# AdaLN block with chunked attention and a routed feed-forward: side pieces on two PSUM banks, routing weights spread by the load

## What is computed

```python
h = layernorm(x) * (1 + ca) + sa
# attention: 16 heads of 128, chunks of 64 rows
q, k, v = h @ q_w.T + q_b, h @ k_w.T + k_b, h @ v_w.T + v_b
beta = softplus(h @ b_w.T + b_b)
out = ((l2norm(q) @ l2norm(k).T) * decay_mask) @ (beta * v)      # inside a chunk
x = x + ga * ((out * silu(h @ og_w.T)) @ o_w.T + o_b)
# feed-forward: 16 experts of 176 columns, top 6 of a softmax, and a shared expert of 352
h = layernorm(x) * (1 + cb) + sb
p = softmax(h @ gate_w.T); w = top6(p) / sum(top6(p))            # 0 for the other ten
y = sum_e w[:, e] * swiglu_e(h) + swiglu_shared(h)
x = x + gb * y
```

## Time and profile before

| what | value |
|---|---|
| median of 3 runs | 2330.7 us (2329.98 to 2335.05) |
| the profiled execution, its own time | 2331.89 us |
| span of its trace | 2330.2 us |
| PE busy | 2215.1 us (95%), granted clock 0.986 of full |
| DVE, ACT, POOL busy | 58%, 37%, 24% |
| PE idle before the products of the gates | 26.8 us, 20 times |
| attention loop / feed-forward loop | about 30 to 1486 us / 1486 to 2328 us |

### The profile page before, as it was taken

How to read it: one execution, slowest core, us unless ns; L and a number is a source line. 1 busy time by engine, 2 the same in 40 slices (tenths; PEclk the granted TensorE clock), 3 DMA queues, 4 the chain that set the end, 5 groups by cost and what they waited for, 6 DMA issues and landing times.

```text
span 2330.2 us, 32531 instructions
## 1 busy us (share of the span) xinstructions
PE 2215.1 (95%) x11436; PEld 1852.0 (79%) x11436; DVE 1349.6 (58%) x2299; ACT 872.5 (37%) x1484; POOL 547.6 (24%) x543
## 2 busy tenths in 40 slices
PE   7899899999989998989999999899999999999998
PEld 6788788777877777877888888788878888888887
DVE  4566566655665666566657565455555545545554
ACT  3433434444434443344444333233333332233332
POOL 2234334333433333333434444100000000000000
PEclk8999999999999999999999999999999999999999
DMA  8353441453533535423313221144334323423221
GB/s 290 136 173 124 171 123 40 143 155 102 145 96 118 151 97 159 136 85 113 105 60 113 91 94 70 46 149 145 108 119 158 97 98 112 167 97 113 95 95 59
DMA packets 192768, 276.40 MB, mean 119 GB/s; under 512 B 99184, under 2 KB 132960, under 8 KB 192608
## 3 DMA queue, kind: packets, MB, share of 16 engines
q1 hardware_dynamic: 192608, 274.33, 36.7%
HBM read 214.79 MB, written 59.51 MB: 118 GB/s over the span
## 4 chain that ended last, share of the span: by engine, by line
PE 48%; DVE 2%; issue 1%; ACT 1%; DVEq 0%; ACTq 0%
PE proj_ps L635 24%; PE out_ps L635 8%; PE s_ps L911 3%; PE av_ps L911 3%; PE kt_ps L911 3%; PE qt_ps L911 3%; PE s_ps L833 1%; PE av_ps L842 1%; PE qt_ps L819 0%; DVE sumsq L1326 0%; PE kt_ps L824 0%; DVE gated L1338 0%; PE misc_ps L714 0%; ACT gated_hi L1044 0%; DVE scores L1319 0%
## 5 line engine op out<-in xcount | busy, mean ns | idle before, releaser
L635 PE MATMUL proj_ps<-w_qkv,h_t 128*128 128x512 f32 x2304 | 624.3, 410 | 8.4 <-DVE v_sb L1313 2.3
L635 PEld LDWEIGHTS proj_ps<-w_qkv,h_t 128*128 128x128 f32 x2304 | 417.1, 192 | 97.5 <-issue 17.8
L635 PE MATMUL proj_ps<-h_t,w_qkv 128*128 128x512 f32 x1800 | 443.3, 391 | 0.9 <-DVE acc L1358 0.9
L591 POOL TENSOR_TENSOR inv_norm<-guarded,minus_half 128x8 f32<-128x8 f32 x128 | 209.4, 1636 | 873.2 <-DVE guarded L1330 873.2
L635 PEld LDWEIGHTS proj_ps<-h_t,w_qkv 128*128 128x128 f32 x1800 | 336.0, 188 | 71.5 <-issue 2.8
L1030 ACT ACTIVATE q_t<-qt_ps 128x512 f32<-128x512 f32 x128 | 76.5, 597 | 425.1 <-PE qt_ps L819 424.9
L635 PE MATMUL proj_ps<-h_t,w_gate 128*128 128x512 f32 x768 | 197.7, 408 | 29.0 <-ACT gate L1050 26.8
L635 PEld LDWEIGHTS proj_ps<-h_t,w_gate 128*128 128x128 f32 x768 | 143.1, 193 | 71.4 <-ACT gate L1050 36.7
L1313 DVE TENSOR_TENSOR q_sb<-proj_ps,bias 128x512 f32<-128x512 f32 x128 | 88.3, 690 | 191.3 <-PE proj_ps L635 178.9
L1326 DVE TENSOR_REDUCE sumsq<-squares 128x8 f32<-128x1024 f32 x128 | 155.6, 1216 | 23.5 <-DVE stage L1234 13.4
L635 PE MATMUL out_ps<-gated_hi,w_out 128*128 128x512 f32 x512 | 159.0, 392 | 3.1 <-ACT gated_hi L1044 2.2
(11 more groups left out here) (183 smaller groups left out, 3094.8 us busy)
## 6 DMA issues: line engine op xcount, KB each, us to landing
w_qkv<-tile_scr SPq DMA_DIRECT2D x100, 768.0 KB, 4.3
w_qkv<-head_scr SPq DMA_DIRECT2D x45, 1024.0 KB, 11.0
head_scr<-stage SPq DMA_DIRECT2D x30, 512.0 KB, 3.0
w_gate<-head_scr SPq DMA_DIRECT2D x15, 1024.0 KB, 4.9
w_out<-head_scr SPq DMA_DIRECT2D x15, 1024.0 KB, 6.7
tile_scr<-stage SPq DMA_DIRECT2D x25, 512.0 KB, 3.2
x_in<-_attn_hidden_states_dram SPq DMA_DIRECT2D x16, 512.0 KB, 5.5
h_scr<-stage SPq DMA_DIRECT2D x16, 512.0 KB, 3.2
```

What stands on the lines that cost most here:

```text
L591: pool.tensor_tensor(inv_norm[b][:, :], guarded[b][:, :], minus_half[:, :], ALU.pow).then_inc(inverted, 1)
L635: mm = pe.matmul(out, w, y, start=(j == 0 and m == 0), stop=(3 * j + m == n - 1))
```

## The change

Three things are changed.

- **Two banks.** A chunk in the second place of a unit with `t` 3 or 0 now uses `out_ps`, which the output products leave alone from their read-out in the `t == 2` unit to the next `t == 2` unit. All other chunks keep `misc_ps`. Each bank has a count of its own; the first output product waits for the chunks of `out_ps`, and such a chunk for the adds that read the last output products.
- **No chunk of a weight or of the routing in (n, 1) with `t == 1`**, in front of the gate products. The routing takes the places one after the other and leaves that one out, so from `turn` on its pieces stand one place later. `prep` and `tile` leave it out too. The input of the second supertile of a quarter is started at unit 32q+22 and no longer at 32q+24, by which its `turn` leaves (n, 1) with `t == 1` and its `soft2` enters it.
- **No `spread`.** `wturn`'s 16 rows are stored, and the load repeats each row eight times. The product L681, the copy L992 and the constant are gone; six routings have these in the unit loop and two in the feed-forward loop. `weights_t` lies in `h_f` now.

```diff
-    def route(s, put, at):
-        put(*at(0), "delta", s)
...
-        put(*at(11), "wturn", s)
-        put(*at(12), "spread", s)
+    def route(s, put, places):
+        for task in (("delta", s), ("x1", s, 0), ("x1", s, 1), ("stats", "f", s), ("norm", "f", s), ("turn", "f", s, 0),
+                     ("turn", "f", s, 1), (("split", "f", s), ("logits", s)), ("prob", s), ("pick", s), ("weigh", s),
+                     ("wturn", s)):
+            at = next(places)
+            for part in task if isinstance(task[0], tuple) else (task,):
+                put(*at, *part)
+
+    def from_unit(n):
+
+        while True:
+            yield n, 0
+            if n % TS != 1:
+                yield n, 1
+            n += 1
...
-            route(2 * (q - 1) + a, put, lambda r, n=32 * q - 1 + 8 * a: (n + r // 2, r % 2))
+            route(2 * (q - 1) + a, put, from_unit(32 * q - 1 + 8 * a))
...
-            first_norm(2 * (q + 1) + a, 32 * q + 18 + 6 * a)
-    chunks = ("turn", "beta", "x1", "logits", "wturn", "spread", "prep", "tile")
-    free = lambda n, p: not any(t[0] in chunks for t in side[n, p])
+            first_norm(2 * (q + 1) + a, 32 * q + 18 + 4 * a)
+    free = lambda n, p: (n % TS, p) != (1, 1) and not any(t[0] in CHUNKS for t in side[n, p])
...
+        second = {t for n in range(N) if n % TS in (3, 0) for t in side[n, 1] if t[0] in CHUNKS}
+        bank_at = {t: sum((v in second) == (t in second) for v in list(chunk_at)[:j]) for t, j in chunk_at.items()}
+        side_bank = {t: (out_ps, side_freed[1]) if t in second else (misc, side_freed[0]) for t in chunk_at}
+        added_by = {t: (n + 1) // TS - 1 for n in range(N) for t in side[n, 1] if t in second}
...
-                elif t[0] == "spread":
+                elif t[0] == "wturn":
                     s = t[1]
-                    sp.wait_ge(combined, s + 1)
-                    sp.dma_start(comb_scr[s], comb_out).then_inc(comb_stored, 16)
+                    sp.wait_ge(weights_copied, s + 1)
+                    sp.dma_start(comb_scr[s], weights_t).then_inc(comb_stored, 16)
...
-                    sp.dma_start(combine[q % 2][:, a, :], comb_scr[s]).then_inc(comb_loaded[q % 2], 16)
+                    sp.dma_start(combine[q % 2][:, a, :], comb_scr[s].unsqueeze(1).broadcast_to([E, ER, ST]))\
+                      .then_inc(comb_loaded[q % 2], 16)
...
             def chunk(task):
-                j = chunk_at[task]
-                after(pe, misc_free, j)
+                after(pe, side_bank[task][1], bank_at[task])
+                if task in second:
+                    after(pe, added, 2 * added_by[task])
+                return side_bank[task][0]
...
                 after(pe, added, 2 * i + k)
+                if k == 0:
+                    after(pe, side_freed[1], second_by[min(TS * (i + 1) + 2, N)])
```

More of the change, by code:

```diff
@@ L39 @@
 Q, K, V, G, O = range(5)
+CHUNKS = ("turn", "beta", "x1", "logits", "wturn", "prep", "tile", "final")
 NI = NQ * NG * 2
@@ L125, in plan @@
     for a in range(2):
-        route(2 * (NQ - 1) + a, lambda u, _, *task: late[u].append(task), lambda r, a=a: (2 + 30 * a + 2 * r, 0))
+        route(2 * (NQ - 1) + a, lambda u, *task: late[u].append(task), ((u,) for u in range(2 + 28 * a, NU, 2)))
     for q in range(NQ):
@@ L279, in build @@
         order += [("final", NQ - 1, a, half) for a in range(2) for half in range(2)]
-        CHUNKS = ("turn", "beta", "x1", "logits", "wturn", "spread", "prep", "tile", "final")
         chunk_at = {t: j for j, t in enumerate(t for t in order if t[0] in CHUNKS)}
+        second = {t for n in range(N) if n % TS in (3, 0) for t in side[n, 1] if t[0] in CHUNKS}
+        bank_at = {t: sum((v in second) == (t in second) for v in list(chunk_at)[:j]) for t, j in chunk_at.items()}
+        side_bank = {t: (out_ps, side_freed[1]) if t in second else (misc, side_freed[0]) for t in chunk_at}
+        added_by = {t: (n + 1) // TS - 1 for n in range(N) for t in side[n, 1] if t in second}
+        second_by = [sum(t in second for v in range(n) for p in range(2) for t in side[v, p]) for n in range(N + 1)]
         norm_at = {t[1:3]: j for j, t in enumerate(t for t in order if t[0] == "norm")}
@@ L556, in _ @@
             pool.memset(causal[:, :], 1.0)
-            pool.memset(prob_ext[:, :, E:E + 2], 2.0)
-            pool.memset(spread[:, :], 1.0).then_inc(made, 1)
+            pool.memset(prob_ext[:, :, E:E + 2], 2.0).then_inc(made, 1)
             pool.wait_ge(made, 1)
@@ L675, in do @@
                         mm = pe.transpose(misc[0:E, t * P:(t + 1) * P], picked[:, t, :], ident)
[L676 to L681 removed]
+                    mm.then_inc(side_filled, 1)
                 elif kind == "prep":
@@ L707, in do @@
                     _, q, a, half = task
-                    chunk(task)
+                    misc = chunk(task)
                     for h in range(KC):
@@ L930, in do @@
                 kind = task[0]
+                misc, freed = side_bank.get(task, (None, None))
                 if kind == "turn":
@@ L1122, in do @@
                     if before:
-                        dve.wait_ge(misc_filled, chunk_at[("turn", *before[0], 1)] + 1)
+                        dve.wait_ge(side_filled, chunk_at[("turn", *before[0], 1)] + 1)
                     for t in range(TS):
```

102 lines of the change are left out of this document (37 added, 65 removed).

## The result

| kernel | median | ratio to before, 95% interval |
|---|---|---|
| before (six runs beside the change) | 2331.89 us | |
| changed | 2316.53 us (2313.95 to 2323.69, six runs) | 0.9937 [0.9923, 0.9951] |

The change makes the kernel 0.6% faster, about 15 us. I had forecast 0.9%, 21 us: the sign is right and the gain three quarters of it. The profiled execution took 2316.73 us, with a span of 2315.0.

The account below looks back on a forecast made before the run. PE, busy 2215.1 of 2330.2 us, was taken to bound the kernel. Terms -25 - 9 + 3 + 12 - 1.6 = -20.6 gave 2311.3 profiled, 2310 us median; forecast 2303 to 2318 (0.49), 8-in-10 range 2294 to 2327.

Parts of the forecast that it names:

- preparation, 1 to 4: Weight preparation in units 0 to 6: bank waits partly go, about 2 in units 0/1 included; gain 6.5 us.
- gates without a piece: Gate products with no chunk in front: the Silu comes earlier in six routings and units 5, 9, 17, 21; gain 9 us.
- softplus and what is behind: Softplus of supertiles 3, 5, 7 moves to the gates, costing 8.7 us, while units behind gain; net +3 us.
- routing, the rest of its units: Routing without the spread product, but with everything behind `turn` one place later; net cost +12 us.
- Pieces across a unit boundary: From (n, 1) to (n+1, 0), two banks remove waits at turn, beta, tiles and weight preparation; gain 25 us.
- The reasoning on unit 4: With the bank's wait gone, PE stands at the V product until DVE's Q bias ends at 81.4; 2.3 us remain gained.
- go to others at the same PE time: Pieces losing the place in front of the gates move to other places with unchanged PE time.
- The routing chain is not the bound: Rival: with Exp load earlier or DVE catching up, routing gains some 8 us instead of losing 12; 2290, chance 0.15.
- The waits come back as bias waits: Rival: bank waits return before V products; 2321 if a third of the gain returns, 2327 if half; chance 0.22.
- the sign that I had set: Waits for `v_sb`, `q_sb` and masked scores growing by more than 15 us in total would show waits returning.
- Slower: Rival: DVE stays late behind the routing and two new waits per routing put PE on the lower clock; 2338, chance 0.07.
- nothing changes: Rival: the bank is no limit and the time stays within 0.2%; chance 0.07.

Follow-up runs that it names:

- soft_new: `banks` with only the earlier start of supertiles 3, 5 and 7, which puts their Ln in front of gate products; 2288.2 us.
- banks: The changed kernel without its change of places: old places, two PSUM banks, no spread product; 2285.2 us.
- pair: The changed kernel with the routing's `logits` on `out_ps`, no longer sharing a bank with the second half of `turn`; 2317.6 us.
- reload_free: `banks` with later Ln for supertiles 2, 4, 6, tiny Silus reloading the table early, and prep and tile kept out of places before gates; 2271.5 us.
- exp_early: The changed kernel plus one tiny Exp on ACT behind the copies of split, so the Exp table loads early; 2312.8 us.

## Why the prediction was right, term by term

The direction and the time were right: 2316.5 us lies in the range and in the forecast's own 2303 to 2318. It lies there narrowly: the same kernel once more, as after2, took 2319.3 us. The sum was -20.6 us; the loop and the feed-forward part of the trace together show -11.8 (the other -3.4 of the span is the start, which goes with the clock). By terms, in us, from the intervals of after against before:

| term | forecast | measured |
|---|---|---|
| turn pairs, intervals 19, 51, 83 | -9 | -10.1 |
| beta behind them, 20, 52, 84 | -3 | -1.4 |
| tiles, 40, 64, 72 | -4.7 | -6.6 |
| preparation, 1 to 4 | -6.5 | -6.2 |
| preparation, 8, 11, 16 | -2 | -3.1 |
| gates without a piece, 5, 9, 17, 21 and the routings' six | -9 | -8.3 |
| softplus and what is behind, 23 to 32, 53, 55 to 63, 85, 87 to 96 | +3 | +5.0 |
| routing, the rest of its units | +12 | +13.2 |
| feed-forward half | -1.6 | -2.5 |
| displaced weight pieces, 6, 10, 18, 22 | 0 | +5.8 |
| a load waited for, interval 12 | 0 | +2.3 |

- **Pieces across a unit boundary: right.** -27.4 against -25. The reasoning on unit 4, that the bank's wait turns in part into one for the Q bias, held: its V product waited 1.7 us for it and interval 3 gained 3.3 (2.3 said). The parts of the preparation's term were less good than its total: the 2 us of units 0/1 lie ahead of the first row, in the start, where two waits for the bank of 2.13 and 2.09 us became 1.51 for the V bias and 2.10 for the Q bias, so that nearly nothing was gained; intervals 3 and 4 made up for it.
- **Gates and softplus: right, with the sizes.** Waits of 3.42 to 3.44 us stand at the gates of units 25, 57 and 89, as said, and those of units 33, 41, 65 and 73 are gone. The softplus' +5.0 is +3.9 in after2, and `soft_new` gives +3.0 for this part alone.
- **Routing: right in mechanism, and in size by two misses that cancel.** The routing's intervals are 13.2 us longer in the changed kernel, where I had forecast 12; but the four routings with tiles took 4.8 of it (6.4 said) and the two without 8.4 (5.6 said). In `rows`, which has only the spread product taken out, these intervals are 11.3 us shorter than before, and in `banks` 19.2: so on two banks the new places cost them some 32 us, far more than the +12 suggests. The Q bias came 4.2 us behind `gated` (4.3 said), the V product waited 1.46 (2.1 said), `wturn` 2.23 (2.8 said). One reason was wrong: I put the wait of `logits` down to `turn` and `logits` sharing `misc_ps`. `pair` shows that it is a wait for ACT's data.
- **The step that failed** is the sentence that the pieces that lose their place in front of the gates "go to others at the same PE time". In the four intervals they went to they cost 5.8 us, their own PE time (0.4 us each by the prediction) included; 4.0 of it is in interval 22, where two of them came to stand on one bank across a boundary and PE waits 2.51 us. `reload_free`, which moves nothing else, shows it too: 5.0 us in interval 22, and a loss of 4.0 over the eight intervals that lose or get a piece. I had named this very pattern for `t == 2` and not looked where the change makes it anew. The plan's places can be listed before a run, and I should have done it for the pieces moved only by the rule for free places. Interval 12 (PE waits 2.25 us for the load of a weight block) is the second omission. `banks`, with the old places, has +2.0 there as well, in waits for biases behind a copy of ACT that itself waits 5.2 us for a store. Both are waits for a DMA; that they come from PE's being earlier is likely and not tested.
- **Rivals.** "The routing chain is not the bound" is out: the three waits stand in every routing. "The waits come back as bias waits" held in a small part: waits for the Q bias are 14.4 us, of which some 8.3 in the routings, which the forecast had in another term. But it was close to the sign that I had set: the waits for Q bias, V bias and masked scores grew from 10.6 to 25.1 us, by 14.5, and above 15 I would have called this rival right. With the routings' 8.3 in it the sign could not tell the two apart; the pieces across a boundary, which gained all that was forecast, do. "Slower" and "nothing changes" are out by the time. Of the slow clock that "slower" reckoned with, the half behind `wturn` is there (2.91 us for six products), the half behind the Q bias' wait of 1.46 us is not (1.66). The rule of the Trainium skill that I weighed (ScalarE: Activation LUTs, What ACT_TABLE_LOAD costs: a load of 1.28 us and a drain of 1.38) isn't borne out in its second half: in unit 57 the Ln ends at 690.76, the load runs from 690.78 to 692.06, and the Silu starts at 692.07. `exp_early` took one load out of each routing's chain, and DVE's Q bias came 1.27 us nearer to `gated`: the load alone, with nothing for a drain.

The forecast was right for this change and blind for what lay beside it: that the same two banks in the old places give 37 us. Every term above was costed against the kernel before, none against the change with one part left out.

## What to carry to other kernels

When several edits come together, cost each of them also as the one left out; a part that was made for another's sake may be worth less than nothing. Between steps of a chain that is worked off in fixed places, it is the distance that counts, not the number of places: moving all by one place made three neighbours of what had been a unit apart, and moving them by two, with the bank rule to match, gave it back. In a stream that switches activation tables, a tiny activation in an idle stretch chooses where the load stands; look at the next user of the old table too, or the load only moves there.

## What the runs showed of the hardware

- **A table load does not wait for its activation's input.** It is issued in the engine's order, as soon as what stands in front is done. In the changed kernel the load for `soft1` of supertile 5 ends four microseconds before the Exp that needs it, which waits for DVE:

```profile
678.53 1.28 ACT L964 ACT_TABLE_LOAD   x1
683.69 0.26 ACT L964 ACTIVATE soft<-soft 128x64 f32<-128x64 f32 x1 [3.87 <-DVE soft L1151]
```

  So it costs only what stands in front of it too late, and one activation of 128x1, 0.20 us, moves it.
- **Some DVE work takes longer beside POOL's.** `gated_lo`, a DVE tensor_tensor of 128x512 with both inputs in SBUF, takes 0.68 us when POOL is idle (the row at 441.06 above) and 1.49 us when it starts together with POOL's work on `q_sb` and the row scales. In the timeline of the changed kernel, unit 57:

```profile
688.77 1.04 POOL L593 TENSOR_TENSOR q_sb<-q_sb,inv_norm 128x512 f32<-128x512 f32 x1
688.88 1.49 DVE L1341 TENSOR_TENSOR gated_lo<-gated,gated_hi 128x512 fp32r<-128x512 f32 x1 [0.70 <-ACT gated_hi L1038]
689.77 0.65 POOL L597 TENSOR_TENSOR v_scale<-inv_norm,beta 128x4 f32<-128x4 f32 x1
```

  It ends at 690.37, when POOL's second operation does (690.42). In the whole trace the 40 of the 128 `gated_lo` that overlap no work of POOL take 0.67 to 0.69 us, and of the 88 that do some are as quick and others reach 1.56. The 384 biases, which read PSUM, take 0.68 to 0.69 us all the same. No run here changed this, so it is read, not tested.
- **The loop repeats, the start doesn't.** Two traces of the changed kernel agree in 1412 us to 0.1 and differ by 4.4 us before it, with a granted clock of 0.92 and 0.84 up to there and nearly the same idle time of PE.
